# Scores in attention: one-hot rows against relation and mask rows as one product of 128 weight columns

## The chip, the cores and the metric

The kernel runs on one core of one Trainium2 chip. The metric is the time of one execution in microseconds on the device, without the profiler; smaller is better.

## What is computed

The reference runs two graph layers over the same 6250 nodes of 256 features and 200 000 edges, sorted by destination. The first is attention over the edges (4 heads of 64); the second sums messages by edge type and mixes the six sums of each node by attention. The part that matters here is the first layer's scores and what is made of them:

```python
mod_k = K[src] + 0.2 * rel[:, None, :]            # rel = rel_w[edge_relations], 64 relations
scores = jnp.einsum('ehd,ehd->eh', Q[dst], mod_k) / D ** 0.5
seg_max = jax.ops.segment_max(scores, dst, num_segments=N)
ex = jnp.exp(scores - seg_max[dst])
agg = jax.ops.segment_sum((ex / denom[dst])[:, :, None] * V[src], dst, num_segments=N)
```

All of it is in float32.

## The kernel before

Four stages follow one another, with barriers between them. `prepare_phase` computes queries, keys and values of all nodes, sorts out which edges belong to which window of destination nodes, and writes tables of counts. `attend_phase` is the first layer's attention. `update_phase` normalizes and computes what the second layer gathers. `relate_mix_phase` is the second layer.

In `attend_phase` the destination nodes stand in windows of 32 (`WQ`), so that 32 nodes x 4 heads fill 128 rows. The edges go in chunks of 128 (`C0`), each belonging to one window, and 4 chunks (`CH`) make a group; there are `GN` = 440 groups, 1760 chunks. Every engine runs through the groups in a loop whose body holds 8 of them (`run`), and they meet by semaphores alone:

- GpSimd (`gather`, L800) fetches the key and value rows of a chunk's 128 sources with one indirect DMA, four for a group, into a ring of 8 groups (`kv`). Before it fills a place again it waits for `o_ps`, the last product that read it.
- TensorE (`group` at L934) does, for group u: `turn_shares` of group u-2 (L919, four transpositions), `turn_keys` of group u+1 (L897, eight transpositions), `scores` of group u (L909 and L912), `weigh` of group u-2 (L929), in this order, the order written out by hand.
- VectorE does `one_hots` (L1034), `take_shares` (L1044, which L929 waits for), `take_keys` (L1039), `maxima` (L1051 to L1061, behind the scores) and `merge` (L1077, four, behind L929).
- ScalarE does `take_keys` (L961), `queries` (L978: copies the window's queries and its relation and mask rows, 256 columns, into `own`), `exps` (L985, L991), and loads rows and register values.
- SyncE loads windows into `rec` and stores finished sums.

In `scores`, the output `p_s` of a chunk has 128 rows (32 nodes x 4 heads) and 128 columns (the chunk's edges). `own[:, o, P:2 * P]` holds, for each of the 128 output rows, the product of its query with the 64 relations (partitions 0 to 63) and a large negative mask for nodes that an edge doesn't belong to (partitions 64 to 127); `hot` holds for each edge two ones, one for its relation and one for its destination node. Their product (L909) adds relation term and mask. `own[:, o, 0:P]` against the turned keys `kt` (L912) adds the query-key product. L912 is by nature two products, since heads 0 and 1 take their keys from other rows than heads 2 and 3: k = 0 gives output rows 0 to 63 and k = 1 rows 64 to 127, each with 64 weight columns, in two column tiles of the array. L909 is cut the same way, although both halves multiply the same `hot`.

The tables of counts (`need`, `ends`, `need0`, `rneed0`, `ends0`) are read as register values by ScalarE and SyncE, which wait on semaphores for them.

Of the kernel before, what the change touches and what calls it, by code (L numbers as in the profile page):

```python
# [1 line left out]

# [3 lines left out]
ALU = mybir.AluOpType  # L19
ACT = mybir.ActivationFunctionType  # L20
AXX = mybir.AxisListType.X
F32 = mybir.dt.float32
BF16 = mybir.dt.bfloat16
I32 = mybir.dt.int32

P = 128
N = 6250
# [15 lines left out]
NQ = NB * P // WQ  # L43
# [8 lines left out]
NU = N // UN  # L52
NW = NU * SBW
# [7 lines left out]
G0, G1 = -(-K0 // P), -(-(K1 + 24) // P)  # L61
# [48 lines left out]
def prepare_phase(nc, a, t):  # L110

    with ExitStack() as ctx:
        s = Scope(nc, ctx, "pre", give_back=True)
        src1 = s.sb("src1", [P, G1 * P], I32)
        row1 = s.sb("row1", [P, G1 * P])
        keep = s.sb("keep", [P, G1 * P])
        need = s.sb("need", [P, G1 * P], I32)
        ends = s.sb("ends", [P, NW], I32)
        before = s.sb("before", [P, NW], I32)  # L120
        slot = s.sb("slot", [P, NW], I32)
        ubase = s.sb("ubase", [1, NU, 2], I32)
# [27 lines left out]
        start = s.sb("start", [P, 2, GB1])  # L150
# [18 lines left out]
        rngrow = s.sb("rngrow", [P, G1 * P + 1])  # L169
        win = s.sb("win", [1, G0 * P])  # L170
        win_i = s.sb("win_i", [1, G0 * P], I32)

        w = s.sb("w", [P, 2, 3 * D])
        bqcol = s.sb("bqcol", [P, 2])
# [71 lines left out]
        with nc.Block() as block:  # L246
            @block.vector
            def _(eng):
                v = nc.vector

                def link(ins):

                    eng.wait_ge(dve.sem, dve.up(ins))
                    return dve.n
# [131 lines left out]
                def layer0_lists():  # L386
                    was = t.fresh0[:, :].rearrange("p (c k) -> p c k", k=2)[:, :, 0]
                    eng.wait_ge(iota_done, 6)
                    link(v.tensor_tensor(was[:, 1:G0 * P], rngrow[:, 1:G0 * P], rngrow[:, 0:G0 * P - 1],
                                         ALU.not_equal))  # L390
                    link(v.tensor_scalar(was[:, 1:G0 * P], was[:, 1:G0 * P], -2.0 * BIG, None, ALU.mult))
                    link(v.tensor_scalar(t.need0[:, :], rngrow[0:1, 0:G0 * P], 16.0, 1.0, ALU.mult, ALU.add))
                    link(v.tensor_scalar(win[:, :], rngrow[0:1, 0:G0 * P], float(NQ - 1), None, ALU.min))
                    link(v.tensor_copy(win_i[:, :], win[:, :]))
                    link(v.tensor_scalar(t.rneed0[:, :], win_i[:, :], 2, None, ALU.logical_shift_right))
                    link(v.tensor_scalar(t.rneed0[:, :], t.rneed0[:, :], 32.0, 32.0, ALU.mult, ALU.add))
                    link(v.tensor_scalar(t.rslot0[:, :], win_i[:, :], RING - 1, None, ALU.bitwise_and))
                    link(v.tensor_copy(t.ends0[:, :], tend[0][0:1, 0:NQ]))
                    link(v.tensor_scalar(win_i[:, 0:NQ], tend[0][0:1, 0:NQ], -1.0, None, ALU.add))
                    link(v.tensor_scalar(t.slot0[:, :], win_i[:, 0:NQ], ACCS - 1, None, ALU.bitwise_and))  # L400
# [309 lines left out]
def attend_phase(nc, a, t):  # L710

    with ExitStack() as ctx:
        s = Scope(nc, ctx, "at", give_back=True)
# [9 lines left out]
        own = s.sb("own", [P, 2 * CH, 2 * P])  # L724
        row = [s.sb(f"row{i}", [P, 2 * CH * C0], BF16) for i in range(4)]
        hot = [s.sb(f"hot{i}", [P, CH * C0]) for i in range(2)]
# [14 lines left out]
        p_s = [s.ps(f"p_s{i}", [P, 512]) for i in range(2)]  # L741
# [43 lines left out]
        with nc.Block() as block:  # L785
# [102 lines left out]
            @block.tensor  # L888
            def _(eng):

                def turn_keys(u, j):
                    eng.wait_ge(kv_in[j], (u - j) * 8 + 64)
                    for k, taken in enumerate((kt_low, kt_high)):
                        if past(u, 1):
                            eng.wait_ge(taken, u)
                        for c in range(CH):
                            mm = eng.transpose(p_k[k][:, c * P:c * P + P], kv[j][:, c, P * k:P * k + P], t.ident[:, :])  # L897
                        mm.then_inc(k_ps, 1)

                def scores(u, j):  # L900
                    eng.wait_ge(kt_low, u + 1)
                    eng.wait_ge(kt_high, u + 1)
                    eng.wait_ge(hot_done, u + 1)
                    eng.wait_ge(own_done, u + 1)
                    for c in range(CH):
                        o = CH * (j % 2) + c
                        at = slice(P * c, P * c + P)
                        for k in range(2):
                            eng.matmul(p_s[j % 2][64 * k:64 * k + 64, at], own[:, o, P + 64 * k:P + 64 * k + 64],  # L909
                                       hot[j % 2][:, at], start=True, stop=False)  # L910
                        for k in range(2):
                            mm = eng.matmul(p_s[j % 2][64 * k:64 * k + 64, at], own[:, o, 64 * k:64 * k + 64],  # L912
                                            kt[j % 2][:, k, c, :], start=False, stop=True)
                    mm.then_inc(s_ps, CH)

                def turn_shares(u, j):
                    eng.wait_ge(ex_done, u + 1)
                    for c in range(CH):
                        mm = eng.transpose(p_t[j % 2][:, P * c:P * c + P], ex[j % 4][:, c, :], t.ident[:, :])  # L919
                    mm.then_inc(turned, 1)  # L920

                def weigh(u, j):
                    eng.wait_ge(pt_done, u + 1)
                    for b in range(2):
                        if past(u, 1):
                            eng.wait_ge(acc_done, u * CH - CH + 2 * b + 2)
                        for c in range(2 * b, 2 * b + 2):
                            for k in range(2):
                                mm = eng.matmul(p_o[b][64 * k:64 * k + 64, VE * (c % 2):VE * (c % 2) + VE],  # L929
                                                pt[j % 2][:, c, 64 * k:64 * k + 64],  # L930
                                                kv[j][:, c, D + VE * k:D + VE * k + VE], start=True, stop=True)
                        mm.then_inc(o_ps, 1)

                def group(u, j, m):  # L934
                    if past(u, BEHIND):
                        turn_shares(u - BEHIND, (j - BEHIND) % U)
                    if exists(u + 1) and exists(u) and not (isinstance(u, int) and u + 1 == GN):
                        turn_keys(u + 1, (j + 1) % U)
                    if exists(u):
                        scores(u, j)  # L940
                    if past(u, BEHIND):
                        weigh(u - BEHIND, (j - BEHIND) % U)
                eng.wait_ge(cleared, 5)
                turn_keys(0, 0)
                run(eng, group)
# [545 lines left out]
def relate_mix_phase(nc, a, out, t):  # L1491

    with ExitStack() as ctx:
        s = Scope(nc, ctx, "rm")
# [8 lines left out]
        src = s.sb("src", [P, G1 * P], I32)  # L1504
        row = s.sb("row", [P, G1 * P])
        keep = s.sb("keep", [P, G1 * P])
        need = s.sb("need", [1, G1 * P // 5], I32)
        ends = s.sb("ends", [1, NW], I32)
        slot = s.sb("slot", [1, NW], I32)
        ubase = s.sb("ubase", [1, 2 * NU], I32)  # L1510
        idx = s.sb("idx", [P, IR], I32)
# [53 lines left out]
        hot = s.sem("hot")  # L1565
# [644 lines left out]
def resnorm_gnn(nc, a, out):  # L2210
    with ExitStack() as ctx:
        s = Scope(nc, ctx, "g")
        t = Tensors()
        t.pads = {n: nc.dram_tensor(f"pad_{n}", [EPAD], I32, kind="Internal").ap()
                  for n in ("src", "dst", "edge_type_6", "edge_type_64")}
# [3 lines left out]
        t.q0 = nc.dram_tensor("q0", [NQ * P, P], F32, kind="Internal").ap()  # L2219
        t.r0 = nc.dram_tensor("r0", [NQ * R64, P], F32, kind="Internal").ap()  # L2220
        t.tables1 = [nc.dram_tensor(f"tables1_{k}", [P if k < 3 else 1, width], dt, kind="Internal").ap()
                     for k, (dt, width) in enumerate(((I32, G1 * P), (F32, G1 * P), (F32, G1 * P), (I32, G1 * P),
                                                      (I32, NW), (I32, NW), (I32, 2 * NU)))]
        t.x1 = nc.dram_tensor("x1_rows", [NB * P, D], F32, kind="Internal").ap()

        t.tx = nc.dram_tensor("tx_rows", [NB * P * R6, D], F32, kind="Internal").ap()
# [11 lines left out]
        with ExitStack() as layer0:  # L2238
            s0 = Scope(nc, layer0, "g0")
            t.src0 = s0.sb("src0", [P, G0 * P], I32)  # L2240
            t.fresh0 = s0.sb("fresh0", [P, 2 * G0 * P])
            t.need0 = s0.sb("need0", [1, G0 * P], I32)
            t.rneed0 = s0.sb("rneed0", [1, G0 * P], I32)
            t.rslot0 = s0.sb("rslot0", [1, G0 * P], I32)
            t.ends0 = s0.sb("ends0", [1, NQ], I32)
            t.slot0 = s0.sb("slot0", [1, NQ], I32)
            prepare_phase(nc, a, t)
            t.wo = s0.sb("wo", [P, 2, D])
            t.gamma, t.beta, t.bo = (s0.sb(n, [P, D]) for n in ("gamma", "beta", "bo"))
            t.bv = s0.sb("bv", [P, 2])  # L2250
            t.wr = s0.sb("wr", [P, 2, R6 * D])
            t.br = s0.sb("br", [P, R6 * D])
            t.ux = [s0.sb(f"ux{i}", [P, D]) for i in range(3)]
            t.uvown = [s0.sb(f"uvown{i}", [P, D]) for i in range(3)]
            t.uw_in = s.sem("uw_in")
            t.ux_in = [s.sem(f"ux_in{i}") for i in range(3)]
            attend_phase(nc, a, t)
            update_phase(nc, a, t)
# [27 lines left out]
```

## Time and profile before

| | |
|---|---|
| median of 3 runs, unprofiled | 5463.11 us (5462.03 to 5466.88) |
| span of the profiled execution | 7316.7 us |
| busy in it: TensorE, its weight loads | 5674.8 us, 4231.9 us |
| busy in it: VectorE, ScalarE, GpSimd | 4006.7 us, 2651.7 us, 3696.3 us |
| L909, L912 matmuls (7040 each) | 764.2 us, 743.0 us busy |

The profiled execution is a third longer than the unprofiled ones. Its durations and steps in stretches without gaps can be used; its waits must be read with care. "issue" in the profile is time in which an engine waited for nothing that the profile shows. A matmul's end is modelled, so starts are compared rather than durations. "128*64" behind an instruction is the part of the array that it uses (rows*columns), "128x128" the output (partitions x elements).

### The profile page before, as it was taken

Reading aid. Unit: us, or ns where it says so; the run is one execution under the profiler, and the core shown is the slowest. Engines: PE = TensorE matmul, PEld = TensorE weight load, DVE = VectorE, ACT = ScalarE, POOL = GpSimd, SP = SyncE. Lnnn points to the kernel's source line nnn. Section 1 sums busy time; section 2 is a strip of 40 time slices with the busy share of each in tenths; the row PEclk is TensorE's granted clock in tenths of the full one; section 3 lists DMA queues with packets and bytes.
Section 4 is the critical chain, followed back from the end, with each engine's and each line's share of the span. In section 5 each row is a group of like instructions: output and inputs, shape, how many; then the busy total and the mean of one; then the engine's idle time right before and its main releaser. Section 6 shows DMA issues by size and latency. Waiting matters only on the chain. (4 is left out here: it accounts for less than half of the span.)

```text
span 7316.7 us, 142121 instructions
## 1 busy us (share of the span) xinstructions
PE 5674.8 (78%) x41507; PEld 4231.9 (58%) x41507; DVE 4006.7 (55%) x12046; ACT 2651.7 (36%) x9038; POOL 3696.3 (51%) x3942
## 2 busy tenths in 40 slices
PE   5767777777777777777797688888878788787888
PEld 3356666666666666666553355556656565555666
DVE  4345555555555555555685455555555555555553
ACT  3434444444444444444321133332323233333334
POOL 2255555555555555555344655555555555555550
PEclk8889999989999999998898788888889888889988
DMA  5576666666666666667565444443434434344431
GB/s 137 159 196 172 175 175 172 173 176 175 173 173 175 173 174 174 172 171 166 128 203 163 117 118 118 116 123 108 124 109 121 118 109 122 110 119 119 116 115 34
DMA packets 615779, 1055.40 MB, mean 144 GB/s; under 512 B 150117, under 2 KB 399547, under 8 KB 615504
## 3 DMA queue, kind: packets, MB, share of 16 engines
q0 software_dynamic: 233984, 716.19, 35.8%
q1 hardware_dynamic: 232374, 181.93, 8.3%
q10 hardware_dynamic: 149210, 155.22, 7.3%
q14 instruction: 171, 1.40, 0.1%
q8 instruction: 40, 0.66, 0.0%
HBM read 913.94 MB, written 142.26 MB: 144 GB/s over the span
## 5 line engine op out<-in xcount | busy, mean ns | idle before, releaser
L1709 POOL DMA_INDIRECT rm_xg<-tx_rows,rm_idx x1875 | 1785.1, 952 | 1413.2 <-PE rm_pa L1740 823.1
L800 POOL DMA_INDIRECT at_kv<-kv_rows,at_idx x1760 | 1673.5, 951 | 1559.9 <-PE at_p_o L929 1028.3
L1740 PE MATMUL rm_pa<-rm_xg,rm_oh 128*126 128x256 f32 x3750 | 1246.9, 451 | 557.6 <-DVE rm_acc L2067 435.3
L2067 DVE SCALAR_TENSOR_TENSOR rm_acc<-rm_acc,rm_kp,rm_pa 126x256 f32<-126x256 f32 x1875 | 897.6, 479 | 858.4 <-PE rm_pa L1740 450.0
L1740 PEld LDWEIGHTS rm_pa<-rm_xg,rm_oh 128*126 128x126 f32 x3750 | 711.9, 212 | 942.2 <-DVE rm_acc L2067 526.2
L929 PE MATMUL at_p_o<-at_kv,at_pt 128*64 128x129 f32 x7040 | 750.5, 293 | 630.0 <-issue 549.9
L985 ACT ACTIVATE at_ex<-at_p_s,at_ntop 128x128 f32<-128x128 f32 x1760 | 503.2, 369 | 1377.2 <-DVE at_ntop L1059 1245.0
L929 PEld LDWEIGHTS at_p_o<-at_kv,at_pt 128*64 128x64 f32 x7040 | 491.9, 142 | 854.2 <-issue 838.9
L1051 DVE TENSOR_REDUCE at_cmax<-at_p_s 128x4 f32<-128x512 f32 x440 | 303.8, 690 | 1101.9 <-DMA rows<-pre_rows_b 1055.1
L909 PE MATMUL at_p_s<-at_hot,at_own 128*64 128x128 f32 x7040 | 764.2, 292 | 40.8 <-issue 39.8
L912 PE MATMUL at_p_s<-at_kt,at_own 128*64 128x128 f32 x7040 | 743.0, 283 | 67.1 <-issue 66.7
L1894 ACT ACTIVATE rm_pr<-rm_psc,rm_ntop 126x126 f32<-126x126 f32 x1200 | 422.9, 365 | 842.5 <-DVE rm_ntop L2094 388.8
L1077 DVE SCALAR_TENSOR_TENSOR at_acc<-at_acc,at_fac,at_p_o 128x129 f32<-128x129 f32 x1760 | 611.6, 348 | 93.7 <-remote 31.0
L978 ACT ACTIVATE at_own<-at_rec 128x256 f32 x1760 | 584.5, 404 | 116.2 <-issue 106.7
L897 PE MATMUL at_p_k<-g_ident,at_kv 128*128 128x128 f32 x3520 | 551.6, 309 | 49.4 <-DMA at_kv<-kv_rows,at_idx 34.0
L1752 PE MATMUL rm_pq<-rm_xt,rm_wt 128*128 128x504 f32 x1200 | 570.2, 598 | 5.8 <-issue 5.8
L2086 DVE TENSOR_REDUCE rm_top<-rm_psc 126x2 f32<-126x252 f32 x600 | 223.4, 414 | 614.3 <-remote 413.5
L909 PEld LDWEIGHTS at_p_s<-at_hot,at_own 128*64 128x64 f32 x7040 | 457.4, 144 | 140.3 <-issue 138.1
L912 PEld LDWEIGHTS at_p_s<-at_kt,at_own 128*64 128x64 f32 x7040 | 487.6, 144 | 84.6 <-issue 84.5
L897 PEld LDWEIGHTS at_p_k<-g_ident,at_kv 128*128 128x128 f32 x3520 | 485.5, 163 | 54.4 <-issue 50.6
L961 ACT ACTIVATE at_kt<-at_p_k,at_bk 128x512 f32<-128x512 f32 x440 | 304.4, 692 | 334.9 <-DMA pre_rows_i<-pad_edge_type,pre_e0i 155.8
L2057 DVE TENSOR_SCALAR rm_oh<-g_iota,rm_rw 128x126 f32<-128x126 f32 x1875 | 403.5, 290 | 0.0
(250 smaller groups left out, 7364.4 us busy)
## 6 DMA issues: line engine op xcount, KB each, us to landing
at_row<-rows ACTq DMA_DIRECT2D x440, 128.0 KB
agg_rows<-rm_acc SPq DMA_DIRECT2D x300, 126.0 KB
rm_st<-agg_rows ACTq DMA_DIRECT2D x75, 504.0 KB
rm_srow<-agg_rows ACTq DMA_DIRECT2D x75, 504.0 KB
tx_rows<-up_tx SPq DMA_DIRECT2D x49, 768.0 KB, 3.6
rm_xg<-tx_rows,rm_idx POOLq DMA_INDIRECT x1875
at_kv<-kv_rows,at_idx POOLq DMA_INDIRECT x1760
sums<-at_acc SPq DMA_DIRECT2D x196, 64.5 KB
```

Of the source, the lines that this page charges most:

```text
L800: eng.indirect_dma_start(out=kv[j][:, c, :], out_offset=None, in_=t.kv, in_offset=bass.IndirectOffsetOnAxis(ap=idx[:, o:o + 1], axis=0),). ...
L897: mm = eng.transpose(p_k[k][:, c * P:c * P + P], kv[j][:, c, P * k:P * k + P], t.ident[:, :])
L909: eng.matmul(p_s[j % 2][64 * k:64 * k + 64, at], own[:, o, P + 64 * k:P + 64 * k + 64], hot[j % 2][:, at], start=True, stop=False)
L912: mm = eng.matmul(p_s[j % 2][64 * k:64 * k + 64, at], own[:, o, 64 * k:64 * k + 64], kt[j % 2][:, k, c, :], start=False, stop=True)
L929: mm = eng.matmul(p_o[b][64 * k:64 * k + 64, VE * (c % 2):VE * (c % 2) + VE], pt[j % 2][:, c, 64 * k:64 * k + 64], kv[j][:, c, D + VE * k: ...
L978: ins = act(own[:, o, :], rec[:, bass.ds(held["slots"][k], 1), :].rearrange("p a c -> p (a c)"), ACT.Copy)
L985: ins = act(ex[j % 4][:, c, :], p_s[j % 2][:, P * c:P * c + P], ACT.Exp, bias=ntop[j % 2][:, c:c + 1])
L1077: v.scalar_tensor_tensor(acc[:, o, :], acc[:, (o - 1) % ACCS, :], fac[j % 4][:, c:c + 1], p_o[c // 2][:, VE * (c % 2):VE * (c % 2) + VE], ...
L1709: eng.indirect_dma_start(out=xg[:, q % XR, :], out_offset=None, in_=t.tx, in_offset=bass.IndirectOffsetOnAxis(ap=idx[:, q % IR:q % IR + 1] ...
L1740: eng.matmul(p_a[q % BANKS][0:WR, 0:D], oh[:, q % OR, :], xg[:, q % XR, :], start=True, stop=True).then_inc(summed, 1)
L1752: mm = eng.matmul(p_q[:, 0:QP], wt[:, k, c, :], xt[piece][:, k, :], start=(k == 0), stop=(k == 1))
L2067: v_.scalar_tensor_tensor(acc[:, q % AR, :], acc[:, (q - 1) % AR, :], kp[0:WR, q % AR:q % AR + 1], p_a[q % BANKS][0:WR, 0:D], ALU.mult, AL ...
```

## The change

In `scores` the two products of 64 weight columns with `hot` become one of 128 weight columns for each chunk, into the whole of `p_s`'s 128 rows; the two products with the keys stay in their two column tiles and add to it. Besides, five tables of counts are kept as unsigned 16-bit instead of 32-bit integers, and one conversion is written to a tile of its own (`rload_i`) instead of in place.

```diff
@@ scores, TensorE
-                        for k in range(2):
-                            eng.matmul(p_s[j % 2][64 * k:64 * k + 64, at], own[:, o, P + 64 * k:P + 64 * k + 64],
-                                       hot[j % 2][:, at], start=True, stop=False)
+                        eng.matmul(p_s[j % 2][:, at], own[:, o, P:2 * P], hot[j % 2][:, at], start=True, stop=False)
                         for k in range(2):
                             mm = eng.matmul(p_s[j % 2][64 * k:64 * k + 64, at], own[:, o, 64 * k:64 * k + 64],
                                             kt[j % 2][:, k, c, :], start=False, stop=True)
@@ prepare_phase, VectorE
-                    link(v.tensor_scalar(t.rneed0[:, :], win_i[:, :], 2, None, ALU.logical_shift_right))
-                    link(v.tensor_scalar(t.rneed0[:, :], t.rneed0[:, :], 32.0, 32.0, ALU.mult, ALU.add))
+                    link(v.tensor_scalar(rload_i[:, :], win_i[:, :], 2, None, ALU.logical_shift_right))
+                    link(v.tensor_scalar(t.rneed0[:, :], rload_i[:, :], 32.0, 32.0, ALU.mult, ALU.add))
@@ tables
-        need = s.sb("need", [P, G1 * P], I32)
-        ends = s.sb("ends", [P, NW], I32)
+        need = s.sb("need", [P, G1 * P], U16)
+        ends = s.sb("ends", [P, NW], U16)
...
-            t.need0 = s0.sb("need0", [1, G0 * P], I32)
-            t.rneed0 = s0.sb("rneed0", [1, G0 * P], I32)
+            t.need0 = s0.sb("need0", [1, G0 * P], U16)
+            t.rneed0 = s0.sb("rneed0", [1, G0 * P], U16)
...
-            t.ends0 = s0.sb("ends0", [1, NQ], I32)
+            t.ends0 = s0.sb("ends0", [1, NQ], U16)
```

The same types are given to the second layer's copies of `need` and `ends` and to the two tables in memory between them.

## Rows read from the trace of the kernel before

**Rows 1.** The page's first line.
```profile
span 7316.7 us, 142121 instructions
```

**Rows 2.** Busy time by windows: window, length; each engine's busy us (instructions); clock, DMA share, GB/s.
```profile
383.00:3585.00 3202.00, 2432.16 (x26382) 1993.06 (x26384) 1849.79 (x4940) 1393.34 (x4395) 1660.88 (x1747) 0.92 0.64 173
```

**Rows 3.** Waits, 500 to 3500 us: waiter <- releaser: us in total, times, longest.
```profile
PEld at_p_o L929 <- issue: 808.3, 1116, 2.0
```

**Rows 4.** Timeline of TensorE, end of attention: start, length, what, how many in one row.
```profile
3562.90 1.04 PE L897 MATMUL at_p_k<-g_ident,at_kv 128*128 128x128 f32 x8
3563.87 0.44 PE L909 MATMUL at_p_s<-at_hot,at_own 128*64 128x128 f32 x4
3564.14 0.39 PE L912 MATMUL at_p_s<-at_kt,at_own 128*64 128x128 f32 x4
3564.35 0.39 PE L909 MATMUL at_p_s<-at_hot,at_own 128*64 128x128 f32 x4
...
3564.79 0.39 PE L909 MATMUL at_p_s<-at_hot,at_own 128*64 128x128 f32 x4
...
3566.68 0.66 PE L919 MATMUL at_p_t<-g_ident,at_ex 128*128 128x128 f32 x4
3567.17 1.04 PE L897 MATMUL at_p_k<-g_ident,at_kv 128*128 128x128 f32 x8
3568.14 0.44 PE L909 MATMUL at_p_s<-at_hot,at_own 128*64 128x128 f32 x4
```

**Rows 5.** Timeline of VectorE, the same stretch: its group's first operation, twice.
```profile
3560.24 0.48 DVE L1034 TENSOR_SCALAR at_hot<-at_row,at_col 128x512 f32<-128x512 bf16 x1
...
3564.51 0.48 DVE L1034 TENSOR_SCALAR at_hot<-at_row,at_col 128x512 f32<-128x512 bf16 x1
```

**Rows 6.** Busy time by windows, the same stretch (PE, PEld, DVE, ACT, POOL).
```profile
3560.00:3574.00 14.00, 12.82 (x181) 11.49 (x179) 13.27 (x36) 9.97 (x32) 0.00 (x0) 1.00 0.11 30
```

**Rows 7.** Timeline of GpSimd at the start of attention: gathers 1, 32 and 33.
```profile
366.39 0.95 POOL L800 DMA_INDIRECT at_kv<-kv_rows,at_idx  x1 [43.20 <-DVE at_idx L1027]
...
405.22 0.95 POOL L800 DMA_INDIRECT at_kv<-kv_rows,at_idx  x1 [0.30 <-issue]
419.50 0.95 POOL L800 DMA_INDIRECT at_kv<-kv_rows,at_idx  x1 [13.33 <-PE at_p_o L929]
```

**Rows 8.** Timeline of GpSimd: attention's last gather, the mix stage's first and last.
```profile
3555.64 0.95 POOL L800 DMA_INDIRECT at_kv<-kv_rows,at_idx  x1 [0.30 <-issue]
...
3946.23 1.00 POOL L1709 DMA_INDIRECT rm_xg<-tx_rows,rm_idx  x1 [0.58 <-issue]
...
7143.03 0.95 POOL L1709 DMA_INDIRECT rm_xg<-tx_rows,rm_idx  x1 [0.30 <-issue]
```

**Rows 9.** Timeline of TensorE in the first stage: products of 128 weight columns.
```profile
31.73 1.06 PE L575 MATMUL pre_pq<-pre_enh,pre_w 128*128 128x128 f32 x8
32.62 0.59 PE L581 MATMUL pre_pkv<-pre_w,pre_enh 128*128 128x512 f32 x1
```

**Rows 10.** Timeline of TensorE's weight loads, end of attention; in brackets the idle before.
```profile
3566.68 0.42 PEld L919 LDWEIGHTS at_p_t<-g_ident,at_ex 128*128 128x128 f32 x4 [0.17 <-issue]
...
3568.14 0.20 PEld L909 LDWEIGHTS at_p_s<-at_hot,at_own 128*64 128x64 f32 x4 [0.17 <-issue]
```

**Rows 11.** Timeline of TensorE, mix stage: L1740 behind products in row tiles (L1770).
```profile
5006.40 1.13 PE L1740 MATMUL rm_pa<-rm_xg,rm_oh 128*126 128x256 f32 x4
5007.36 0.59 PE L1752 MATMUL rm_pq<-rm_xt,rm_wt 128*128 128x504 f32 x1
```

**Rows 12.** Timeline of TensorE, mix stage: L1740 behind L1752, the whole array before and after.
```profile
4198.70 1.03 PE L1740 MATMUL rm_pa<-rm_xg,rm_oh 128*126 128x256 f32 x4
4199.56 0.84 PE L1797 MATMUL rm_pm<-rm_gd,rm_pr 126*126 126x21 f32 x7
```

**Rows 13.** Busy time by windows, gathers at full pace alone.
```profile
390.00:400.00 10.00, 1.66 (x5) 0.90 (x5) 0.00 (x0) 0.00 (x0) 7.59 (x8) 0.56 0.77 210
```

**Rows 14.** Groups of instructions: line, operation, count, busy us, mean ns, idle before.
```profile
L396 DVE TENSOR_SCALAR g_rneed<-g_rneed 1x1792 int32<-1x1792 int32 x1 | 1.1, 1082 | 0.0
```

More of the change, by code:

```diff
@@ L24 @@
 I32 = mybir.dt.int32
+U16 = mybir.dt.uint16
 P = 128
@@ L171, in prepare_phase @@
         win_i = s.sb("win_i", [1, G0 * P], I32)
+        rload_i = s.sb("rload_i", [1, G0 * P], I32)
         w = s.sb("w", [P, 2, 3 * D])
@@ L1506, in relate_mix_phase @@
         keep = s.sb("keep", [P, G1 * P])
-        need = s.sb("need", [1, G1 * P // 5], I32)
-        ends = s.sb("ends", [1, NW], I32)
+        need = s.sb("need", [1, G1 * P // 5], U16)
+        ends = s.sb("ends", [1, NW], U16)
         slot = s.sb("slot", [1, NW], I32)
@@ L2221, in resnorm_gnn @@
         t.tables1 = [nc.dram_tensor(f"tables1_{k}", [P if k < 3 else 1, width], dt, kind="Internal").ap()
-                     for k, (dt, width) in enumerate(((I32, G1 * P), (F32, G1 * P), (F32, G1 * P), (I32, G1 * P),
-                                                      (I32, NW), (I32, NW), (I32, 2 * NU)))]
+                     for k, (dt, width) in enumerate(((I32, G1 * P), (F32, G1 * P), (F32, G1 * P), (U16, G1 * P),
+                                                      (U16, NW), (I32, NW), (I32, 2 * NU)))]
         t.x1 = nc.dram_tensor("x1_rows", [NB * P, D], F32, kind="Internal").ap()
```

## The prediction

> **What bounds the kernel now.** I read the page's head first [rows 1]: the profiled span is 7316.7 us where the unprofiled median is 5463.11. So 1854 us of the profiled execution are not there when nobody records, and no share of its span may be carried over. The stages [rows 2] and the waits in attention [rows 3] say what the extra is. Between the landmarks of the trace, attention takes 3202 us, 7.28 us for each of its 440 groups of four chunks, and there TensorE, VectorE, ScalarE and GpSimd all wait, TensorE mostly for "issue" (808 us before the loads of L929 alone), nothing that the profile shows. I take these waits for the recording's own, and look for stretches without them.
>
> At the end of attention, when all gathers have been issued, TensorE [rows 4] and VectorE [rows 5] show three groups without a gap at full clock [rows 6]: a group begins with L909 at 3563.87 and again at 3568.14, 4.27 us, and VectorE's begins at 3560.24 and 3564.51, 4.27 us too. That is what these two engines need for a group. GpSimd needs more. The gathers' starts at full pace [rows 7]: from 366.39 to 405.22 there are 31 steps, 1.2526 us each; then the ring of 32 is full and GpSimd waits for L929. Four gathers are 5.01 us a group. I go by starts, not by the 0.95 us durations; by the Trainium skill, Perfetto Trace Analysis, section Per-engine timelines, a GpSimd span should be treated as unreliable and start-to-start spacing used, and here the 0.30 us of idle "issue" behind each gather belongs to its price.
>
> A check on that reading, from rows alone: to the first gather 366.4 us [rows 7]; 1760 gathers x 1.2526 = 2204.6; from the last of them, 3555.64, to the first gather of the mix stage, 3946.23, 390.6 [rows 8]; 1875 x 1.2526 = 2348.6; from its last, 7143.03, to the end of the span 173.7 [rows 1, 8]. The sum is 5483.9, 21 us (0.4%) over the unprofiled median. Were attention bound by TensorE and VectorE, 440 x 4.27 = 1879 us would stand for 2205 and the sum would miss by 305. So attention runs at GpSimd's pace, 5.01 us a group, and TensorE has 5.01 - 4.27 = 0.74 us a group to spare. The change is worth nothing until it has used these 0.74 us up.
>
> **The change part by part.** *The product itself.* Before, each chunk has two products of 64 weight columns in two column tiles. A product in float32 is two loads and two matmul instructions, so L909 x4 stands in a chunk, and L912 x4 behind it; L909 and L912 together take 0.44 us (3564.35 to 3564.79) [rows 4], 0.11 us for each pair of instructions that run side by side in the two halves. After, the chunk has two instructions of 128 columns instead of four of 64. The nearest row of that shape is L575, 128*128 with 128x128 of float32: eight in 0.89 us (31.73 to 32.62), 0.11 us each [rows 9]. So 2 x 0.11 replaces 2 x 0.11: the array's work is the same, 0.22 us a chunk. Eight loads and eight matmul instructions a group go away (of 60 and 60), 3520 of each in all; the undisturbed stretch has no gap for them to fill, so I price that at nothing. If it were a gain, it would be that of rival four.
>
> *The switches.* The product of 128 columns uses the array whole, L912 behind it uses it in two column tiles, and the next chunk's product uses it whole again. Before, a group changes only twice: L897 to L909, and L929 to L919. What one costs stands in the same rows. To the tiles: L897 x8 should take 0.87 us at 0.11 each and takes 0.97 (3562.90 to 3563.87), and the first L909 x4 take 0.27 where later ones take 0.22 [rows 4]: 0.10 + 0.05 = 0.15 us. The weight load shows why: at both kinds of change it starts only with its matmul, after 0.17 us of idle, and not ahead as otherwise [rows 10]. Back to the whole array, the same idle 0.17 us is seen, so again 0.10 us for emptying; for the load of 128 columns that then lies bare the nearest row is L1740 behind the row-tiled L1770: four instructions in 0.96 us (5006.40 to 5007.36) [rows 11] against 0.86 (4198.70 to 4199.56) without a change [rows 12], 0.10 us. L919, a transposition, shows less: 0.49 for four at 0.11, 0.05 us [rows 4]. I take 0.10, because L1740 is a plain float32 product as the new one is; so 0.20 us back, bounds 0.15 and 0.20.
>
> The first chunk's product follows L897, which is whole already: its change only moves from before L909 to before L912. Chunks two to four add one change each way, 3 x (0.15 + 0.20) = 1.05 us a group; the change at the group's end stays. TensorE's group becomes 4.27 + 1.05 = 5.32 us. With the transposition's 0.05 it is 5.17; with emptying alone (6 x 0.10) 4.87.
>
> By the Trainium skill, TensorEngine Tiling (Array Packing), section Key Properties, changing the tiling mode drains the engine, while changing the tile alone does not. It gives no price; the rows do. TensorE: Matmul & The Clock Gate, section Step-by-step, says on the other side that a weight load is pulled ahead of matmuls in flight when it goes to the background buffer. If that held across a change, the loads would not lie bare and the sum would be that with emptying alone; the 0.17 us of idle say that it does not hold there.
>
> *What follows in the kernel.* TensorE's order in a group is L919, L897, the scores, L929. The scores grow, so L929 comes later, and with it what waits for it: VectorE's four L1077 (1.56 us) and the buffer that GpSimd's gather eight groups on takes. VectorE needs 4.27 us and ScalarE about 3.4 (9.97 us in 14 us, 3.28 groups of 4.27, give 3.04, plus its waits) [rows 6], both below 5.32, and L1044, for which L929 waits, can run while the longer scores do. So after the change TensorE is last, with 5.32 against GpSimd's 5.01: the first 0.74 us of 1.05 are hidden by the gathers, 0.31 is on the path. 440 x 0.31 = 136 us. The DMA engines are no bound: at the gathers' full pace they are 77% busy with the gathers alone (390 to 400 us) [rows 13], and at a slower pace this only gets easier.
>
> *The tables in 16 bits.* The counts in need, ends and rneed are written as 16-bit and not 32-bit integers; one conversion goes to a tile of its own instead of in place. The same number of operations, of about 1.1 us each, once [rows 14]; ScalarE's and SyncE's register loads from them stay as many. The transfers of two tables halve, once, in the first stage, beside three of 960 KB. Bounds -3 and +3 us; I take 0.
>
> **Sum.** The profiled span cannot carry the sum, since its groups take 7.28 us. Against my reconstruction it is 5483.9 + 136 = 5620; I add the difference to the unprofiled median: 5463 + 136 = 5599 us, 2.5% longer.
>
> **The rivals.** *One: all hidden, 5463 us.* It is so if six changes cost under 0.74 us, 0.12 each. For it: with emptying alone it is 0.60, and what lies bare in a load may be less between products whose weights come from one tile. Against it: both kinds of change show a second, slower step in every stretch that I read. Chance 0.13.
>
> *Two: none hidden, 5463 + 440 x 1.05 = 5925 us.* It is so if TensorE or its loop with VectorE bounds attention already in the unprofiled run, so that the whole 1.05 counts. For it: both engines need the same 4.27 us and are tightly laced. Against it: the check above would miss by 305 us. Chance 0.07.
>
> *Three: a clock that falls.* While the array empties so often, the granted clock, 1.00 in the undisturbed stretch [rows 6] and 0.92 over attention [rows 2], may spend some time at its lower level (1.2 GHz and not 2.4), where a group costs up to twice as much. A twentieth of the time there is 0.27 us a group, 117 us more: 5716. It belongs to the upper end of the forecast. Chance 0.07.
>
> *Four, on the other side: TensorE's instruction stream is a bound in the unprofiled run too.* The waits called issue (808 us before the loads of L929) [rows 3] would not all be the recording's, and 16 fewer of 120 instructions a group would shorten them, at changes cheaper than 0.10 us together. It decides from the point where attention in the unprofiled run is above GpSimd's 2205 us. Were the other stages (366 + 391 + 174 = 931 us) a tenth shorter unprofiled, some 90 us of the median would be such waits; more than these it can't gain, GpSimd's pace is the floor: 5463 - 90 = 5373 us. Chance 0.05.
>
> **How the numbers follow.** Forecast 0.68, rivals 0.13, 0.07, 0.07, 0.05. The range takes the forecast with its bounds (5.17 gives +70, so 5533; 5.32 gives 5599), reaches down to the hidden case, because any price between 0.12 and 0.15 a change lies on the way to it, and up to most of rival three: 5458 to 5710. Outside are rivals two and four and half of three, 0.155. A measurement can tell some 0.2%, 11 us, from no change: slower 0.82 (forecast, two, three), same 0.13, faster 0.05.
>
> **What would show it.** In the profile after, at the end of attention, a group of TensorE 5.2 to 5.35 us long with no idle but the changes; L909 x2 with 128*128, then L912 x4, 0.78 us a chunk for 0.44; VectorE with gaps of 1 us in each group there, before L1051; GpSimd at 5.01 for the 32 gathers at the start as before. The profiled span itself may go either way. Wrong would be: a chunk under 0.64 us (rival one), or unprofiled time beyond 5750 with that same chunk (rival two), or a clock much under 0.92 in attention (rival three).

## The result and the profile after

| | us | |
|---|---|---|
| before, median | 5462.57 | 5461.35 to 5466.88 |
| after, median | 5573.92 | 5572.80 to 5577.36 |
| after, span of the profiled execution | 5571.0 | clock 0.972 |

The ratio is 1.0204, interval 1.0189 to 1.0218: the changed kernel is 111 us slower. 136 us were forecast.

The page of after: its first line, the busy time of each engine, and two of the groups (line, engine, operation, shapes, count; busy us and mean ns; idle before). The product of the one-hot rows is L897 now and the one with the keys L899.

```profile
span 5571.0 us, 135081 instructions
PE 5254.8 (94%) x37987; PEld 3898.6 (70%) x37987; DVE 3997.5 (72%) x12046; ACT 2670.4 (48%) x9038; POOL 3736.6 (67%) x3942
...
L897 PE MATMUL at_p_s<-at_hot,at_own 128*128 128x128 f32 x3520 | 818.5, 314 | 3.6 <-DVE at_kt L1026 2.0
L899 PE MATMUL at_p_s<-at_kt,at_own 128*64 128x128 f32 x7040 | 776.2, 299 | 0.0
```

The instructions are 7040 fewer than in [rows 1], 3520 loads and 3520 matmuls, as the change says. The profiled span is 3 us below the unprofiled median here; in [rows 1] it was 1854 us above it. That is the first thing that the prediction had not expected, and the section on why comes back to it.

A group on TensorE in the middle of attention, from the timeline of after (start, length, what, how many); it answers to [rows 4].

```profile
1500.07 0.39 PE L897 MATMUL at_p_s<-at_hot,at_own 128*128 128x128 f32 x2
1500.39 0.44 PE L899 MATMUL at_p_s<-at_kt,at_own 128*64 128x128 f32 x4
1500.76 0.49 PE L897 MATMUL at_p_s<-at_hot,at_own 128*128 128x128 f32 x2
1501.18 0.44 PE L899 MATMUL at_p_s<-at_kt,at_own 128*64 128x128 f32 x4
1501.55 0.49 PE L897 MATMUL at_p_s<-at_hot,at_own 128*128 128x128 f32 x2
...
1503.02 1.05 PE L916 MATMUL at_p_o<-at_kv,at_pt 128*64 128x129 f32 x16
1504.00 0.66 PE L906 MATMUL at_p_t<-g_ident,at_ex 128*128 128x128 f32 x4
1504.50 1.04 PE L886 MATMUL at_p_k<-g_ident,at_kv 128*128 128x128 f32 x8
1505.37 0.39 PE L897 MATMUL at_p_s<-at_hot,at_own 128*128 128x128 f32 x2
```

A chunk goes from 1500.76 to 1501.55, 0.79 us for 0.44 in [rows 4]: 0.42 until the key products start and 0.37 until the next chunk does. A group goes from 1500.07 to 1505.37, 5.30 us, and no row has idle time in brackets. The first chunk's L897 stands behind the transpositions of L886, which use the whole array too, and the key products start 0.32 us after it; behind the later ones they start after 0.42, and the 0.10 more is the load that lies bare, which means that no matmul runs over it. The weight loads of the same stretch show it as [rows 10] did for the two changes that were there before:

```profile
1499.96 0.30 PEld L897 LDWEIGHTS at_p_s<-at_hot,at_own 128*128 128x128 f32 x2
1500.39 0.20 PEld L899 LDWEIGHTS at_p_s<-at_kt,at_own 128*64 128x64 f32 x4
1500.76 0.30 PEld L897 LDWEIGHTS at_p_s<-at_hot,at_own 128*128 128x128 f32 x2 [0.17 <-issue]
```

The first chunk's load of L897 starts at 1499.96, ahead of its matmul at 1500.07. The second chunk's has 0.17 us of idle before it and starts with its own matmul, at 1500.76.

VectorE in the same group (timeline; in brackets idle and what ended it), and GpSimd's gather there:

```profile
1503.24 0.69 DVE L1038 TENSOR_REDUCE at_cmax<-at_p_s 128x4 f32<-128x512 f32 x1 [0.90 <-PE at_p_s L899]
```

```profile
1507.54 0.94 POOL L789 DMA_INDIRECT at_kv<-kv_rows,at_idx  x1 [1.70 <-issue]
```

VectorE waits 0.90 us for the scores, where gaps of 1 us were forecast. GpSimd, which had the longest loop, stands idle 1.70 us before this gather where 0.30 belongs to a gather's price. TensorE has no gap and is last.

### The profile page after: what moved, and what is told of

It reads as the page before. It is cut to its first block and busy times, and to the rows that moved or that the text cites. A ratio compares the mean times of both kernels' runs of the same rounds, so it can differ in the third digit from the quotient of the medians.

```text
span 5571.0 us, 135081 instructions
## 1 busy us (share of the span) xinstructions
PE 5254.8 (94%) x37987; PEld 3898.6 (70%) x37987; DVE 3997.5 (72%) x12046; ACT 2670.4 (48%) x9038; POOL 3736.6 (67%) x3942
## 5 line engine op out<-in xcount | busy, mean ns | idle before, releaser
L789 POOL DMA_INDIRECT at_kv<-kv_rows,at_idx x1760 | 1710.8, 972 | 696.8 <-issue 598.6
L1727 PE MATMUL rm_pa<-rm_xg,rm_oh 128*126 128x256 f32 x3750 | 1060.3, 408 | 117.2 <-DVE rm_acc L2054 53.8
L1727 PEld LDWEIGHTS rm_pa<-rm_xg,rm_oh 128*126 128x126 f32 x3750 | 676.0, 194 | 383.2 <-issue 169.4
L897 PE MATMUL at_p_s<-at_hot,at_own 128*128 128x128 f32 x3520 | 818.5, 314 | 3.6 <-DVE at_kt L1026 2.0
L899 PE MATMUL at_p_s<-at_kt,at_own 128*64 128x128 f32 x7040 | 776.2, 299 | 0.0
L897 PEld LDWEIGHTS at_p_s<-at_hot,at_own 128*128 128x128 f32 x3520 | 527.6, 189 | 232.8 <-issue 230.1
L886 PE MATMUL at_p_k<-g_ident,at_kv 128*128 128x128 f32 x3520 | 460.7, 274 | 70.9 <-DMA at_kv<-kv_rows,at_idx 43.7
L899 PEld LDWEIGHTS at_p_s<-at_kt,at_own 128*64 128x64 f32 x7040 | 349.2, 135 | 213.9 <-issue 2.5
L916 PE MATMUL at_p_o<-at_kv,at_pt 128*64 128x129 f32 x7040 | 465.0, 273 | 3.4 <-DVE at_pt L1031 3.2
L886 PEld LDWEIGHTS at_p_k<-g_ident,at_kv 128*128 128x128 f32 x3520 | 400.5, 142 | 75.1 <-issue 31.0
L916 PEld LDWEIGHTS at_p_o<-at_kv,at_pt 128*64 128x64 f32 x7040 | 403.9, 137 | 4.1 <-DVE at_pt L1031 3.7
```

Source lines behind the costliest of these rows:

```text
L789: eng.indirect_dma_start(out=kv[j][:, c, :], out_offset=None, in_=t.kv, in_offset=bass.IndirectOffsetOnAxis(ap=idx[:, o:o + 1], axis=0),). ...
L897: eng.matmul(p_s[j % 2][:, at], own[:, o, P:2 * P], hot[j % 2][:, at], start=True, stop=False)
L1727: eng.matmul(p_a[q % BANKS][0:WR, 0:D], oh[:, q % OR, :], xg[:, q % XR, :], start=True, stop=True).then_inc(summed, 1)
```

## The experiments

Four kernels were compared with the kernel before on one chip, where before took 5460.2 us (5454.14 to 5467.28, 27 runs). The diffs show what differs from the changed kernel. In the text, the mode of a product is how it uses the array, whole or in column tiles. The count of changes of mode in a group decides what each experiment tells: a pair is one change to the tiles and one back. The kernel before has 1 pair, the changed kernel 4.

**The tables alone.**

```diff
-                        eng.matmul(p_s[j % 2][:, at], own[:, o, P:2 * P], hot[j % 2][:, at], start=True, stop=False)
+                        for k in range(2):
+                            eng.matmul(p_s[j % 2][64 * k:64 * k + 64, at], own[:, o, P + 64 * k:P + 64 * k + 64],
+                                       hot[j % 2][:, at], start=True, stop=False)
```

> The kernel before with the 16-bit tables alone; the products with the one-hot rows stay in two column tiles. Theory A (the 111 us come from the changes between whole array and column tiles, of which only what goes beyond GpSimd's pace counts): 5463 us, within 3. Rival R3 (the tables, through register loads or their transfers, carry part of the 111 us): between 5466 and 5574. Its profile should show attention at GpSimd's pace, about 5.05 us a group, TensorE with 0.7 to 0.8 us idle in each.

Measured: 5460.3 us (5457.0 to 5468.56), ratio 1.0003 (0.9994 to 1.0012). So the 16-bit tables cost nothing, and the 111 us are the product's (the product's change with the tables in 32 bits was not tried). Since this kernel is the kernel before but for the tables, and its profiled span is 5460.4 us, its trace is also the undisturbed view that the trace of before did not give. TensorE, one group (timeline):

```profile
1000.86 0.44 PE L898 MATMUL at_p_s<-at_hot,at_own 128*64 128x128 f32 x4
1001.13 0.39 PE L901 MATMUL at_p_s<-at_kt,at_own 128*64 128x128 f32 x4
1001.35 0.39 PE L898 MATMUL at_p_s<-at_hot,at_own 128*64 128x128 f32 x4
...
1005.10 0.44 PE L898 MATMUL at_p_s<-at_hot,at_own 128*64 128x128 f32 x4
```

4.24 us. Its gathers, GpSimd's timeline, at the start of attention, near its end and around the mix stage (L1698):

```profile
294.74 0.95 POOL L789 DMA_INDIRECT at_kv<-kv_rows,at_idx  x1 [42.90 <-DVE at_idx L1016]
...
398.93 0.95 POOL L789 DMA_INDIRECT at_kv<-kv_rows,at_idx  x1 [0.30 <-issue]
416.05 0.94 POOL L789 DMA_INDIRECT at_kv<-kv_rows,at_idx  x1 [16.18 <-PE at_p_o L918]
...
2457.84 0.95 POOL L789 DMA_INDIRECT at_kv<-kv_rows,at_idx  x1 [11.04 <-PE at_p_o L918]
...
2553.27 0.95 POOL L789 DMA_INDIRECT at_kv<-kv_rows,at_idx  x1 [0.30 <-issue]
...
2953.04 0.99 POOL L1698 DMA_INDIRECT rm_xg<-tx_rows,rm_idx  x1 [0.58 <-issue]
...
5307.49 0.95 POOL L1698 DMA_INDIRECT rm_xg<-tx_rows,rm_idx  x1 [0.30 <-issue]
```

From first to last the gathers of attention take 2258.5 us. At the 1.2526 us a step of [rows 7] they would take some 2204. The other 54 us are nearly all waits of GpSimd for L918, one of 16 us at 416.05 and several from 2433 on, 35.5 us together. Between these GpSimd sets the pace.

**Two chunks of four.**

```diff
-                        eng.matmul(p_s[j % 2][:, at], own[:, o, P:2 * P], hot[j % 2][:, at], start=True, stop=False)
+                        if c in (1, 2):
+                            eng.matmul(p_s[j % 2][:, at], own[:, o, P:2 * P], hot[j % 2][:, at], start=True, stop=False)
+                        else:
+                            for k in range(2):
+                                eng.matmul(p_s[j % 2][64 * k:64 * k + 64, at], own[:, o, P + 64 * k:P + 64 * k + 64],
+                                           hot[j % 2][:, at], start=True, stop=False)
```

Three pairs of changes.

> 16-bit tables, and the product of 128 columns for chunks 1 and 2 of each group's 0 to 3 only: two changes each way more than before instead of three. Theory A: TensorE's group 4.27 + 2 x 0.34 = 4.95 us, still under GpSimd's 5.05, so nothing of it is seen: 5463 us, within 10. Rival R1 (TensorE is on the path already before, and every added change costs in proportion): 5463 + 2/3 of 111 = 5537 us.

Measured: 5467.93 us (5462.19 to 5472.52), ratio 1.0014 (1.0005 to 1.0023). TensorE, one group, from the shares' product to the next one (timeline):

```profile
1500.14 1.05 PE L921 MATMUL at_p_o<-at_kv,at_pt 128*64 128x129 f32 x16
...
1502.86 0.39 PE L904 MATMUL at_p_s<-at_kt,at_own 128*64 128x128 f32 x4
1503.17 0.49 PE L898 MATMUL at_p_s<-at_hot,at_own 128*128 128x128 f32 x2
1503.59 0.44 PE L904 MATMUL at_p_s<-at_kt,at_own 128*64 128x128 f32 x4
1503.96 0.49 PE L898 MATMUL at_p_s<-at_hot,at_own 128*128 128x128 f32 x2
...
1505.09 1.05 PE L921 MATMUL at_p_o<-at_kv,at_pt 128*64 128x129 f32 x16
```

The group has grown from 4.24 to 4.95 us, and the kernel by 8 us. This is the run that shows the slack: 440 x 0.71 = 312 us of new work on TensorE, of which at least 304 are hidden behind GpSimd's 5.01 us a group. In attention itself nearly all of it is hidden: from first to last gather this trace has 2259.6 us and that of tables_only 2258.5, so most of the 8 us lie in stages that the edit doesn't touch. Had every added pair counted (rival R1), the kernel would have taken 5537 us. The two changes of mode cost the same in it as in after (0.42 and 0.37 us a chunk); they cost no time until they are more than the slack.

**Sorted by mode.** All four one-hot products first, then all key products:

```diff
-                        eng.matmul(p_s[j % 2][:, at], own[:, o, P:2 * P], hot[j % 2][:, at], start=True, stop=False)
+                        eng.matmul(p_s[j % 2][:, at], own[:, o, P:2 * P], hot[j % 2][:, at], start=(c == 0), stop=False)
+                    for c in range(CH):
+                        o = CH * (j % 2) + c
+                        at = slice(P * c, P * c + P)
                         for k in range(2):
...
-                                            kt[j % 2][:, k, c, :], start=False, stop=True)
+                                            kt[j % 2][:, k, c, :], start=False, stop=(c == CH - 1))
```

One pair of changes, with the 128-column product and the 3520 fewer matmul instructions kept.

> The changed kernel with the order in scores turned round: all four products of 128 columns first, then the eight with the keys in column tiles, so a group changes twice as before, with 16 loads and matmul instructions fewer in all. Theory A: TensorE's group 4.27 us, GpSimd last, 5463 us, within 5. Rival R4 (the product of 128 columns is dear in itself, not the changes): as the changed kernel, 5574 us.

Measured: 5465.44 us (5455.28 to 5469.09), ratio 1.0008 (0.9999 to 1.0017). TensorE, one group (timeline):

```profile
1340.10 1.06 PE L897 MATMUL at_p_s<-at_hot,at_own 128*128 128x128 f32 x8
1341.09 1.09 PE L902 MATMUL at_p_s<-at_kt,at_own 128*64 128x128 f32 x16
1342.01 1.05 PE L919 MATMUL at_p_o<-at_kv,at_pt 128*64 128x129 f32 x16
1343.00 0.66 PE L909 MATMUL at_p_t<-g_ident,at_ex 128*128 128x128 f32 x4
1343.49 1.04 PE L886 MATMUL at_p_k<-g_ident,at_kv 128*128 128x128 f32 x8
1344.36 1.06 PE L897 MATMUL at_p_s<-at_hot,at_own 128*128 128x128 f32 x8
```

4.26 us, with the same matmuls as after, which takes 5.30. Only the order and with it the start and stop flags differ, so the 1.04 us are the three pairs of changes. It also shows that the 128-column product is neither dearer nor cheaper by itself: the group takes what it took before, and so does the kernel, because GpSimd is the floor.

**Keys first.** The key products of a chunk before its one-hot product:

```diff
-                        eng.matmul(p_s[j % 2][:, at], own[:, o, P:2 * P], hot[j % 2][:, at], start=True, stop=False)
                         for k in range(2):
...
-                                            kt[j % 2][:, k, c, :], start=False, stop=True)
+                                            kt[j % 2][:, k, c, :], start=True, stop=False)
+                        mm = eng.matmul(p_s[j % 2][:, at], own[:, o, P:2 * P], hot[j % 2][:, at], start=False, stop=True)
```

The scores now begin in column tiles, behind transpositions that use the whole array, and they end with the whole array, before the shares' product, which is in column tiles. So the same instructions as in after have five pairs.

> The changed kernel with the products with the keys first in each chunk and the product of 128 columns last: one change each way more than in the changed kernel (five to the tiles and five back, not four and four). Theory A: 0.34 us a group more, TensorE being last the whole of it is seen: 5.30 + 0.34 = 5.64 us a group, 5574 + 151 = 5725 us. Rival R1 (each added pair of changes costs 111/3 us): 5574 + 37 = 5611 us.

Measured: 5710.35 us (5707.75 to 5715.48), ratio 1.0464 (1.0448 to 1.0480). TensorE, one group (timeline):

```profile
1500.49 0.44 PE L898 MATMUL at_p_s<-at_kt,at_own 128*64 128x128 f32 x4
1500.86 0.49 PE L900 MATMUL at_p_s<-at_hot,at_own 128*128 128x128 f32 x2
...
1503.22 0.49 PE L900 MATMUL at_p_s<-at_hot,at_own 128*128 128x128 f32 x2
1503.64 1.10 PE L916 MATMUL at_p_o<-at_kv,at_pt 128*64 128x129 f32 x16
...
1506.13 0.44 PE L898 MATMUL at_p_s<-at_kt,at_own 128*64 128x128 f32 x4
```

5.64 us, 0.34 more than after for one more pair. The kernel is 136 us slower than after's 5573.92 (measured beside a before of 5462.57), close to 440 x 0.34 = 150 and far from the 37 of rival R1: beyond the slack nearly every microsecond counts.

The same stretch of attention, 1000 to 2000 us, in three of these traces, tables_only, after and keys_first (busy time by windows, columns as in [rows 2]):

```profile
1000.00:2000.00 1000.00, 893.73 (x11987) 797.77 (x11987) 829.31 (x2248) 634.57 (x1999) 757.50 (x797) 0.98 0.88 251
```

```profile
1000.00:2000.00 1000.00, 1000.00 (x9816) 778.80 (x9812) 790.51 (x2126) 603.38 (x1889) 734.73 (x755) 1.00 0.84 238
```

```profile
1000.00:2000.00 1000.00, 1000.00 (x9216) 732.79 (x9216) 740.24 (x1993) 565.08 (x1774) 672.23 (x709) 1.00 0.80 224
```

GpSimd's count is four for a group: 797, 755 and 709 give 5.02, 5.30 and 5.64 us a group. TensorE goes from 89% to 100% busy between the first and the second, and its clock stands at 1.00 in after. A bound by gathers that the change holds up (rival R5 below) does not fit this window, in which TensorE never stops and GpSimd has the idle time.

**Three gathers for four.** To see TensorE's own price without GpSimd's floor, the fourth gather of a group is left out once the ring is full:

```diff
-                    for c in range(CH):
+                    for c in range(CH - 1 if past(u, U) else CH):
...
-                    eng.wait_ge(kv_in[j], (u - j) * 8 + 64)
+                    eng.wait_ge(kv_in[j], (u - j) * 6 + 64)
```

It was put into the product as before (with the tables alone), as after and sorted.

> 16-bit tables, products as before, and GpSimd's gather of each group's fourth chunk left out from the ninth group on (the chunk's keys and values stay those of an earlier group, so the first layer's output is another). GpSimd's group falls from 5.05 to about 3.8 us. Theory A: TensorE and VectorE are last with 4.27 us: 5463 - 440 x 0.78 = 5120 us. Rival R1 (TensorE bounds attention before already): 5463 us, no change.

> The changed kernel with the same gather left out. Theory A: TensorE is last with 5.30 us a group and a faster GpSimd gives nothing: 5574 us, within 10; so the change would cost 454 us here (rival two of the prediction in a kernel where it holds) where it costs 111 with all gathers. Rival R5 (the 111 us come from gathers that are held up or slowed by the change): it falls towards 5120 + 111 = 5231 us.

> The sorted order (all products of 128 columns of a group first, then those with the keys) with the same gather left out. Theory A: two changes a group as before, 4.27 us, VectorE's own need, 5120 us, within 15 of before_3g. If fewer loads and matmul instructions were worth something to TensorE, VectorE's 4.27 us would hide it in the time, and it shows in TensorE's idle time alone.

The question was not answered, because these three ran on another chip and the kernel before itself took 7254.88 us on it. Measured: 6628.46, 6546.27 and 6529.32 us, ratios 0.9140 (0.9115 to 0.9166), 0.9037 (0.9011 to 0.9062) and 0.9004 (0.8981 to 0.9028). On a second chip, with the changed kernel beside them, before took 7260.44 us, and on a third, for the first of them alone, 7226.01.

> The same kernel as before_3g, whose three kernels ran where even the kernel before takes 7255 us (its profiled execution of 7317 us was such a one). If this call meets 5460 us for the kernel before, Theory A: 5463 - 440 x 0.78 = 5120 us, rival R1: 5463 us. If it meets 7255 us again, 6628 us.

> The same kernel as after_3g. Where the kernel before takes 5460 us, Theory A: TensorE last with 5.30 us a group, 5574 us, within 10; rival R5 (gathers held up by the change): towards 5231 us. Where it takes 7255 us: 6546 us again.

> The same kernel as sorted_3g. Where the kernel before takes 5460 us, Theory A: 5120 us, within 15 of before_3g_b. Where it takes 7255 us: 6529 us again.

> The changed kernel again. Where the kernel before takes 5460 us: 5574 us. Where it takes 7255 us, TensorE's waits called issue set the time, and 16 of 120 loads and matmul instructions fewer a group make it shorter if these waits go with the number of instructions (rival four of the prediction, in the case in which its condition holds): between 7255 x 6546/6628 = 7165 and 7255 us; if Theory A's changes counted there too, 7255 + 111 = 7366 us or more.

> The same kernel as before_3g, once more, to have it where the kernel before takes 5460 us. There, Theory A: GpSimd's group falls under TensorE's 4.24 us, which is then last: 440 x (5.13 - 4.24) = 392 us less than the kernel before, 5070 us (with the 5.13 us a group that tables_only showed; 5120 with the 5.05 taken before). Rival R1 (TensorE bounds attention before already): 5463 us. Where the kernel before takes 7255 us: 6630 us again.

Measured: 6642.91 us (ratio 0.9162, 0.9122 to 0.9202), 6529.7 (0.9007, 0.8966 to 0.9048), 6496.26 (0.8940, 0.8894 to 0.8987); the changed kernel 7130.76 (0.9827, 0.9780 to 0.9874), less than the 7165 to 7255 expected; the last 6646.91 (0.9197, 0.9156 to 0.9239). So what the three kernels would take where before takes 5460 us stays open. What these runs did show is another thing: on the one of these chips where it ran, the changed kernel is 1.7% faster than the kernel before, not 2% slower. The windows of before, after_b and before_3g_b, 1000 to 2000 us:

```profile
1000.00:2000.00 1000.00, 765.88 (x8282) 627.45 (x8280) 582.29 (x1554) 438.43 (x1380) 524.60 (x553) 0.92 0.63 174
```

```profile
1000.00:2000.00 1000.00, 871.04 (x7565) 644.21 (x7566) 615.90 (x1639) 462.26 (x1455) 553.91 (x582) 0.95 0.66 183
```

```profile
1000.00:2000.00 1000.00, 847.13 (x10416) 697.97 (x10417) 731.91 (x1955) 551.12 (x1739) 493.62 (x521) 1.00 0.63 173
```

By the gathers, a group takes 7.23 us in before and 6.87 in after_b; in before_3g_b, with three gathers a group, 5.76. No engine is full in any of them. The waits of TensorE's loads, 500 to 3300 us, for before and for after_b (waiter <- releaser: us in total, times, longest):

```profile
PEld at_p_o L929 <- issue: 753.7, 1036, 2.0
```

```profile
PEld at_p_o L916 <- issue: 326.3, 414, 2.0
```

This wait falls by more than half. The two traces are no clean pair, though: they were taken apart, and the mix stage, which the change doesn't touch, is 37 us shorter in after_b too. Nor is it shown that the time is gained by this wait. The three kernels with three gathers ran beside one another, and their traces on the second chip, before_3g_b, after_3g_b and sorted_3g_b, have of it (500 to 2800 us):

```profile
PEld at_p_o L918 <- issue: 539.2, 935, 1.7
```

```profile
PEld at_p_o L916 <- issue: 62.7, 192, 0.8
```

```profile
PEld at_p_o L919 <- issue: 490.2, 411, 1.9
```

From first to last gather a group of attention takes 5.79, 5.52 and 5.51 us in them. The sorted kernel has the 16 fewer of 120 TensorE instructions, keeps most of the wait and is as fast as the changed one, which has lost nearly all of it. So this wait is not what sets the time there; that the switches merely fill it would fit, and isn't shown. What the two share is the product of 128 columns with its fewer instructions, and both are faster than the products as before: 82 and 99 us on the first chip, 113 and 147 on the second. The gain goes with that; by which wait is open.

## Why the prediction came out as it did

**The group on TensorE: right.** 5.32 us was worked out, 5.30 measured; the chunk 0.78 and 0.79. The price of the two changes, 0.15 and 0.20 us, was the step most in doubt, its lower bounds being 5.17 and 4.87 for the group. The runs settle it, with 1, 3, 4 and 5 pairs in a group:

| kernel | pairs | group, us |
|---|---|---|
| tables_only | 1 | 4.24 |
| sorted | 1 | 4.26 |
| two_chunks | 3 | 4.95 |
| after | 4 | 5.30 |
| keys_first | 5 | 5.64 |

The steps are 0.34 to 0.36 us a pair throughout. Taking L1740 and not the transposition L919 for the load that lies bare on the way back was the right choice. The Trainium skill, TensorEngine Tiling (Array Packing), section Key Properties, says that changing the mode drains the engine; sorted against after bears that out, 1.04 us for three pairs.

**The product itself, priced at nothing: right** where the stretch is undisturbed: sorted has it, and takes 4.26 us a group for 4.24. On the chips where before takes 7226 to 7260 us it seems to be worth something, as said above.

**GpSimd's pace hides the first part: right in kind, too small in size.** This is the term that was mis-sized. The prediction had 0.74 us of 1.05 hidden and 0.31 on the path, 136 us. The gathers of attention, first to last, in after (GpSimd's timeline):

```profile
294.81 0.95 POOL L789 DMA_INDIRECT at_kv<-kv_rows,at_idx  x1 [42.20 <-DVE at_idx L1014]
...
2659.21 0.95 POOL L789 DMA_INDIRECT at_kv<-kv_rows,at_idx  x1 [0.31 <-issue]
```

2364.4 us against 2258.5 in tables_only: 106 us of the 111 are there, 0.24 us a group for the 0.31 forecast. Two things made it smaller. The group with the change takes 5.30 us and not 5.32, so in the steady stretch 5.30 - 5.01 = 0.29 us a group is on the path, 128 us. And attention before does not run at GpSimd's pace throughout: 2258.5 us is 54 more than 1760 steps of 1.2526, in the waits at 416.05 and near the end, while after has 2364.4 - 440 x 5.30 = 32 us of such time. The difference, 22 us, is given back. 128 - 22 = 106. The prediction had no term for such waits.

**The check that stood for this step** came to 5483.9 us, 21 over the median, and the sum was nearly right while its parts were not:

| part, us | by the prediction | tables_only |
|---|---|---|
| to the first gather | 366.4 | 294.7 |
| gathers of attention | 2204.6 | 2258.5 |
| to the first of the mix stage | 390.6 | 399.8 |
| gathers of the mix stage | 2348.6 | 2354.5 |
| to the end | 173.7 | 153.0 |

The first stage was taken 72 us too long, from a trace of the other kind (in after_b the first gather is at 364.1 us too), and attention 54 too short. That these nearly cancelled was luck. The check could still tell GpSimd's pace from TensorE's (it would have missed by 305 us), and that was all it was needed for.

**The tables at nothing: right**, 1.0003 (0.9994 to 1.0012).

**That the 1854 us are the recording's: wrong.** In after the profiled span is 5571.0 us and the unprofiled median 5573.92, in tables_only 5460.4 and 5460.3. On the other chips it is the same: 7120.6 and 7130.76 in after_b. Recording costs nothing that can be seen. The trace of before, 7316.7 us, looks like the unprofiled executions on the three chips where before takes 7226 to 7260 us, at the same clock: 0.891. The forecast survived this error because its term was worked out from stretches in which nothing waits, and those give 4.27 there and 4.24 here, and because it was added to the unprofiled median and not to a profiled span.

**The rivals.** One (all hidden) falls: a pair costs 0.35 us, and three are over the slack. It is nearly what two_chunks does, 8 us. Two (none hidden, 5925 us) falls by the same run, in which 312 us of new work on TensorE cost 8. Three (a lower clock) falls: 1.00 in the window of after, and the whole kernel's clock rose from 0.957 in tables_only to 0.972. Four (TensorE's instruction stream is a bound in the unprofiled run too) falls where before takes 5460 us, since sorted has the fewer instructions and gains nothing. But what it forecast, a faster kernel, came on the other chips, where attention takes 7.25 us a group and not 5.13: the changed kernel is 1.7% faster on the one where it ran. Its mechanism is not shown: the wait that it named, the one before the loads of the shares' product, is no measure of the time, as sorted_3g_b against after_3g_b says. The prediction gave it 0.05 because it had put [rows 3] down to the recording. This kernel has no one answer: it depends on which of the two kinds of chip it runs on.

## What to carry to other kernels

Order TensorE's products by the way they use the array, and count changes of mode as work: here, in float32 at full clock, a pair costs 0.35 us, and one loop split in two (sorted) saves three of them. Before pricing a change on one engine, work out by how much another engine's pace is slower, since up to there it costs nothing and beyond it nearly all of it counts: 0.71 us more a group cost 8 us in all, 1.06 cost 111 and 1.40 cost 250. A wait that shrinks in a trace is not yet time gained: look for a kernel that keeps the wait and see whether it is slower. And a profile that is a third longer than the unprofiled time is here no recording of the same thing with a burden on it; take it as an execution of another kind, and ask what the change would do in that kind too.

## What the runs showed of the hardware

- Two kinds of chip or of place: the same kernel takes 5460 us on one chip (27 runs within 0.25%) and 7226 to 7260 us on three others. The cause was not found. None of these four chips was seen at two times, so it isn't shown either that it is the chip itself.
- Where before takes over 7200 us, the gathers at full pace start 1.25 us apart [rows 7], as on the chip of 5460, and an undisturbed group takes 4.27 us [rows 4] for 4.24; TensorE's loads and matmuls are late for "issue" at hundreds of places, [rows 3]. That TensorE's instructions come at a fixed highest rate would be the simple reading, and the windows speak against it: before has 8282 matmuls in 1000 us and before_3g_b 10416. Measured over all gathers of attention in four traces (before, before_3g_b, after_b, after_3g_b; the first was taken apart from the others), one gather of four left out takes 1.46 us off a group's 7.25, the 16 fewer instructions 0.37, both together 1.73, so the two add up nearly. The DMA engines move 174, 183 and 173 GB/s in the three windows, nearly the same, and 251 in tables_only. That the instructions and the gathered rows share something on their way would fit; it isn't shown.
- Sorting gains little there with three gathers (6529.32 after 6546.27, 6496.26 after 6529.7 us), although TensorE is less busy (824 for 992 us in 1000 to 2000 us of sorted_3g_b and after_3g_b); what the bound is then stays open. Sorted with all four gathers was not run in such a place.
